# Second expert layer of a routed mixture: the last two of eight weight blocks go from float32 products to split products

## Chip, cores and metric

The kernel runs on one core of a Trainium2 chip. The metric is the device time of one execution in microseconds; a lower one is better. The kernel is one program; nothing is computed on the host but layouts.

## What is computed

The input is four images of 256 channels by 32 x 32 points, which are 4096 tokens of 256 numbers. Three layers follow each other: a convolutional self-attention per image, an eight-head attention per image, and a routed feed-forward layer. The last one, cut to what matters here:

```python
E, D, H = (8, 256, 1024)
route_prob = softmax(xt @ Wr + br)
routes = argmax(route_prob)
h = gelu(xt @ w1 + bb1)              # 256 -> 1024, by the token's own expert
y = h @ w2 + bb2                     # 1024 -> 256: the second expert layer
out = sum over experts of y * (routes == e)
x = t + out
```

The reference runs every expert on every token and masks the result; the kernel sorts the tokens by expert and runs each through its own. All of it is float32.

## The kernel before

The kernel has four phases, each of them a block in which every engine has its own stream of instructions, and which ends when all engines have come to its end.

**conv_phase** works through four images of eight blocks of 128 tokens. TensorE does the projections, the scores and the outputs, VectorE the maxima and the residuals, ScalarE the exponentials. GpSimd adds the normed rows to the residual (`a_res`, L479 and L483) once per image, and in the time left prepares the second layer's weights: `w2_load` brings a piece of 128 x 512 into one of two raw buffers (the memory of `w_qk1`, which is free once VectorE has split it; semaphore `v_wlo`), `w2_split` rounds it to `w2_hi` (type fp32r, L452), subtracts to get the low half in place (L454), and stores both halves to a scratch tensor in memory, `w2_scr`. Six of the eight 256-column blocks of each expert are prepared (`SPLIT = 6`), which is 24 pieces, six per image. `w2_hi` is one buffer: each piece waits until the one before has been stored (`w2_hi_out`). The next load waits for the low half of the other raw buffer (`w2_lo_out`).

**head_phase** works through 32 heads. At every fourth head SyncE's queue loads one expert's `w2_hi` (six blocks, from scratch) and `w2_rest` (blocks 6 and 7, from the input).

**output_phase** projects the values, adds them to the residual (`res0` to `res3`), stores the result (`t_scr`, L1458), norms it, routes it, and scatters each token's normed row to its expert's region (`rows_out`, L1400, one indirect transfer from GpSimd's queue per block of 128 tokens, 32 in all). SyncE's queue loads the low halves (`w2_lo`, L1453) and, into `res0`, the biases `b2`. Tables say which expert and which rows each tile has. Those of the first nine tiles (`READY`) are made from two images alone, so that the expert tiles can start early. At its end SyncE waits for the scatters of these two images (`ready_scattered`) and for the tables, and then issues the rows of tile 0 (`xs`, L1478), the first layer's weights of tile 0 (L1481, one transfer of 1 MB into the memory of `lnt`) and the rows of tile 1.

**expert_phase** works through 39 tiles of 128 rows. The order on TensorE is: first layer of tile i + 1 (L1984, 16 float32 matmuls that are recorded as 32), two transposes of the rows of tile i + 2 (L1973), second layer of tile i. A float32 matmul here is recorded as two. The second layer takes blocks 0 to 5 as three products of fp32r halves (high x high and high x low, L1998; low x high, L2003) and blocks 6 and 7 as float32 matmuls (L2000):

```python
for c in range(SPLIT):
    for w in (w2_hi, w2_lo):
        nc.tensor.matmul(ps_y[:, 0:C], hid_hi[k][:, c, :], of(w, c), ...)
for c in range(SPLIT, KC):
    nc.tensor.matmul(ps_y[:, 0:C], hid_t[k][:, c, :], of(w2_rest, c - SPLIT), ...)
pe.wait_ge(v_lo, i + 1)
for c in range(SPLIT):
    last = nc.tensor.matmul(ps_y[:, 0:C], hid_lo[k][:, c, :], of(w2_hi, c), ...)
```

VectorE's order per tile is: bias of the first layer's result (L1910), copy of the turned rows (`xs_c`, L1917), result `ys` of the tile before (L1928, L1935), low half of the hidden rows (`hid_lo`, L1922). Between its tiles 0 and 1 and its tiles 1 and 2 it also makes the tables of the other 30 tiles (L1333 to L1391). ScalarE does GELU (`hid`, L2035) and the high half (`hid_hi`, L2037). GpSimd gathers the residual rows and scatters the results. SyncE's queue loads rows (L1789) and 1 MB of first-layer weights per tile (L1811 for tile 1, L1795 for the others; the buffer comes free when the first layer two tiles before is done, `pe_hid`), and fills the regions' ends (L1779). All of the latter must have landed, and all scatters, before it loads tile 8.

Of the kernel before, what the change touches and what calls it, by code (L numbers as in the profile page):

```python
# [25 lines left out]
F32R = mybir.dt.float32r  # L26
# [5 lines left out]
P = 128  # L32
# [17 lines left out]
SPLIT = 6  # L50
PIECE = 2 * C
W2_PIECES = E * SPLIT * C // PIECE
# [209 lines left out]
def conv_phase(nc, io, keep, hd):  # L262
# [5 lines left out]
    with ExitStack() as ctx:  # L268
# [56 lines left out]
        w2_in, w2_lo_out = [sem(f"w2_in{k}") for k in range(2)], [sem(f"w2_lo_out{k}") for k in range(2)]  # L325
# [23 lines left out]
        with nc.Block(no_gpsimd_drain=True) as block:  # L349
# [82 lines left out]
            def _(pool):  # L432
# [8 lines left out]
                def w2_load(n):  # L441
                    e, cols = w2_piece(n)
                    pool.dma_start(w2_raw[:, n % 2, :], io["w2"][e][:, cols]).then_inc(w2_in[n % 2], 16)

                def w2_split(n):

                    k = n % 2
                    e, cols = w2_piece(n)
                    pool.wait_ge(w2_in[k], 16 * (n // 2) + 16)
                    if n:  # L450
                        pool.wait_ge(w2_hi_out, 16 * n)
                    nc.gpsimd.tensor_copy(w2_hi[:, :], w2_raw[:, k, :]).then_inc(g_whi, 1)  # L452
                    pool.wait_ge(g_whi, n + 1)
                    nc.gpsimd.tensor_tensor(w2_raw[:, k, :].bitcast(F32R), w2_raw[:, k, :], raw(w2_hi[:, :]), ALU.subtract).then_inc(g_wlo, 1)  # L454
                    pool.dma_start(io["w2_scr"][0, e][:, cols], raw(w2_hi[:, :])).then_inc(w2_hi_out, 16)
                    pool.wait_ge(g_wlo, n + 1)
                    pool.dma_start(io["w2_scr"][1, e][:, cols], w2_raw[:, k, :]).then_inc(w2_lo_out[k], 16)
# [9 lines left out]
                pool.wait_ge(v_wlo, 1)  # L467
                w2_load(0)
                w2_load(1)
                for b in range(B):  # L470
                    r = res[b % 2]
                    for n in range(b * W2_PIECES // B, (b + 1) * W2_PIECES // B):
# [18 lines left out]
                for k in range(2):  # L491
                    pool.wait_ge(w2_lo_out[k], 16 * W2_PIECES // 2)

# [488 lines left out]
def head_phase(nc, io, keep, sems, hd):  # L982


    with ExitStack() as ctx:
# [40 lines left out]
        with nc.Block(no_gpsimd_drain=True) as block:  # L1026

            @block.sync
            def _(sp):
# [3 lines left out]
                def head(t, j, first=False, left=SLOTS):  # L1033
# [3 lines left out]
                    if not first:  # L1037
# [5 lines left out]
                        if j == 2:  # L1043
                            sp.dma_start(raw(keep["w2_hi"][:, bass.ds(t, 1)]).rearrange("p o k m -> p (o k m)"),
                                         io["w2_scr"][0, bass.ds(t, 1)].rearrange("o p m -> (o p) m")).then_inc(sems["w_in"], 16)
# [357 lines left out]

def first_weights(keep):
# [4 lines left out]
def output_phase(nc, io, keep, sems):  # L1409


    with ExitStack() as ctx:
# [32 lines left out]
        with nc.Block(no_gpsimd_drain=True) as block:  # L1445

            @block.sync
            def _(sp):
                for b in range(2, B):
                    res_load(sp, io, keep, sems, b)  # L1450
                def w2_rests(experts):
                    for e in experts:
                        sp.dma_start(raw(keep["w2_lo"][:, e]).rearrange("p k m -> p (k m)"), io["w2_scr"][1, e]).then_inc(sems["lo_in"], 16)  # L1453

                w2_rests(range(6, E))
                for b in range(B):
# [6 lines left out]
                    if b == 1:  # L1463
# [5 lines left out]
                        sp.dma_start(keep["res0"][:, :, :], io["b2"].partition_broadcast(P)).then_inc(sems["bias_in"], 16)  # L1469
                table = keep["schedule"]  # L1470
# [3 lines left out]
                for k, w1 in enumerate(first_weights(keep)):  # L1474
# [242 lines left out]
def expert_phase(nc, io, keep, sems):  # L1717


    with ExitStack() as ctx:  # L1720
# [9 lines left out]
        w2_hi, w2_lo, w2_rest, prior = keep["w2_hi"], keep["w2_lo"], keep["w2_rest"], keep["prior"]  # L1730
# [7 lines left out]
        hid_hi, hid_lo = ([sb(f"hid_{x}{k}", [P, SPLIT, P], F32R) for k in range(2)] for x in ("hi", "lo"))  # L1738
# [42 lines left out]
        with nc.Block() as block:  # L1781
# [115 lines left out]
            def _(dve):  # L1897
# [21 lines left out]
                def rest(i, k):  # L1919

                    dve.wait_ge(a_hi, i + 1)
                    nc.vector.tensor_tensor(hid_lo[k][:, :, :], hid_t[k][:, 0:SPLIT, :], raw(hid_hi[k][:, :, :]), ALU.subtract).then_inc(v_lo, 1)  # L1922

# [27 lines left out]
                rest(0, 0)  # L1951
# [14 lines left out]
            def _(pe):  # L1966
# [21 lines left out]
                def second_layer(i, k, first=False):  # L1988
# [3 lines left out]
                    else:  # L1992
                        pe.wait_ge(sems["lo_in"], 16 * E)
                    of = lambda w, c: w[:, bass.ds(e, 1), c, :].rearrange("p o n -> p (o n)")
# [34 lines left out]
            def _(act):  # L2029
                def gelu(i, k, first=False):  # L2030
# [6 lines left out]
                    nc.scalar.activation(hid_hi[k][:, :, :], hid_t[k][:, 0:SPLIT, :], ACT.Copy).then_inc(a_hi, 1)  # L2037
# [12 lines left out]
def program(nc, io):  # L2050
    for n, shape in (("qk_scr", [2, 2, B * NH, D, N]),
                     ("v_scr", [P, B * NH, NB * D]), ("r_scr", [B, N, C]), ("t_scr", [B * N + P, C]), ("xs_scr", [E * REGION, C + 1]),
                     ("w2_scr", [2, E, P, SPLIT * C])):
        io[n] = nc.dram_tensor(n, shape, F32, kind="Internal").ap()
    with ExitStack() as ctx:
# [11 lines left out]
        keep["w2_hi"] = ctx.enter_context(nc.sbuf_tensor("w2_hi", [P, E, SPLIT, C], F32R))  # L2067
        keep.update(kept((("w2_rest", [P, E, KC - SPLIT, C]), ("padding", [P, C + 1]),
# [13 lines left out]
        keep["w2_lo"] = ctx.enter_context(nc.sbuf_tensor("w2_lo", [P, E, SPLIT, C], F32R))  # L2082
# [57 lines left out]
```

## Time and profile before

| | |
|---|---|
| median of 3 runs | 1191.05 us (1190.48 to 1195.1) |
| the profiled execution, its own time | 1192.07 us |
| its span, first to last instruction | 1190.2 us |
| TensorE busy | 1106.0 us, 93% |
| VectorE / GpSimd / ScalarE busy | 713.0 / 677.9 / 469.7 us |
| mean granted TensorE clock | 0.954 of 2.4 GHz |
| conv_phase | about 0 to 345 us |
| head_phase | about 345 to 832 us |
| output_phase | about 832 to 900 us |
| expert_phase | about 900 us to the end |

Times of instructions are microseconds from the start of the span. A wait is put down to what released it. Matmuls overlap in their pipeline, so the time that one takes of TensorE is the distance between the starts of two, or a group's share of the chain of work, and not the duration of one. "DMA share" is the mean busy share of the 16 DMA engines. The granted clock is told as a share of the full one.

### The profile page before, as it was taken

The numbers are of one execution on the slowest core, as the hardware profiler recorded it, in microseconds if no ns is written. First come the engines' busy times: TensorE is split into PE (matmuls) and PEld (weight loads), VectorE is DVE, ScalarE is ACT, GpSimd is POOL, SyncE is SP. The second block draws the span as 40 slices with busy tenths as digits, with TensorE's granted clock in tenths as the row PEclk, the third lists the DMA queues.
The fourth block names the chain that finished last, engine by engine and source line by source line (L and its number), as shares of the span: only waits on it lengthen the run. The fifth ranks groups of instructions, "written<-read, shape, count | busy, mean of one in ns | idle before, by whom it ended". The sixth has DMA issues, their size and how long they took to land. (4 is left out here: it accounts for less than half of the span.)

```text
span 1190.2 us, 24360 instructions
## 1 busy us (share of the span) xinstructions
PE 1106.0 (93%) x7846; PEld 817.5 (69%) x7847; DVE 713.0 (60%) x1523; ACT 469.7 (39%) x556; POOL 677.9 (57%) x686
## 2 busy tenths in 40 slices
PE   6898999899689999999999999999876999999995
PEld 3586878778455555555555555556756899999995
DVE  3265757657757777777777777760574544444442
ACT  2303232131225555555555555555551222232231
POOL 0155444263337777777777777783057455555553
PEclk8799999989779999999999999999888999999998
DMA  7335465636171323232323232314678666566561
GB/s 218 98 107 182 163 212 182 252 106 221 48 267 40 97 61 97 60 97 62 97 62 97 62 97 62 97 33 125 248 287 254 212 209 229 202 212 220 199 224 36
DMA packets 69677, 173.67 MB, mean 146 GB/s; under 512 B 12768, under 2 KB 33184, under 8 KB 68992
## 3 DMA queue, kind: packets, MB, share of 16 engines
q1 hardware_dynamic: 56336, 131.25, 34.4%
q0 software_dynamic: 13296, 41.84, 10.3%
q8 instruction: 25, 0.41, 0.1%
q14 instruction: 20, 0.16, 0.0%
HBM read 117.16 MB, written 52.45 MB: 143 GB/s over the span
## 5 line engine op out<-in xcount | busy, mean ns | idle before, releaser
L225 DVE TENSOR_REDUCE s_nmax<-ps_v 128x1 f32<-128x512 f32 x484 | 311.6, 686 | 115.9 <-PE ps_v L219 106.4
L1088 POOL TENSOR_TENSOR h_added<-h_added,h_expd 128x1024 f32<-128x1024 f32 x124 | 295.5, 2383 | 38.2 <-ACT h_expd L1111 30.4
L1111 ACT ACTIVATE h_expd<-ps_v 128x1024 f32<-128x1024 f32 x128 | 131.0, 1023 | 154.9 <-PE ps_v L1137 150.2
L1984 PE MATMUL ps_h<-xs_c,lnt 128*128 128x128 f32 x1248 | 149.4, 279 | 5.6 <-DVE xs_c L1917 3.8
L1984 PEld LDWEIGHTS ps_h<-xs_c,lnt 128*128 128x128 f32 x1248 | 146.0, 196 | 6.8 <-issue 4.1
L1151 PE MATMUL h_ps_o<-h_expd,s_vh 128*32 128x256 f32 x2048 | 137.9, 387 | 0.0
L1111 ACT ACTIVATE h_expd<-h_ps_e 128x1024 f32<-128x1024 f32 x128 | 130.4, 1018 | 0.0
L653 PE MATMUL a_ps_v<-a_val,a_expd 128*128 128x257 f32 x512 | 120.6, 389 | 5.8 <-ACT a_expd L524 4.5
L653 PEld LDWEIGHTS a_ps_v<-a_val,a_expd 128*128 128x128 f32 x512 | 98.5, 194 | 24.3 <-ACT a_expd L524 6.5
L2035 ACT ACTIVATE hid<-ps_h 128x1024 f32<-128x1024 f32 x39 | 39.9, 1024 | 188.4 <-DVE ps_h L1910 188.4
L1838 POOL TENSOR_TENSOR pause<-pause 128x1 f32<-128x1 f32 x156 | 53.2, 341 | 103.6 <-DVE ys L1935 92.6
L1088 POOL TENSOR_TENSOR h_added<-h_expd 128x1024 f32<-128x1024 f32 x31 | 73.8, 2380 | 56.4 <-ACT h_expd L1111 56.4
L1910 DVE TENSOR_TENSOR ps_h<-ps_h,b_t 128x1024 f32<-128x1024 f32 x39 | 48.1, 1233 | 87.0 <-PE ps_h L1984 85.6
L1151 PEld LDWEIGHTS h_ps_o<-h_expd,s_vh 128*32 128x32 f32 x2048 | 53.7, 109 | 51.9 <-issue 22.5
L802 DVE TENSOR_REDUCE a_nmax<-a_ps_m 128x1 f32<-128x512 f32 x64 | 41.2, 685 | 63.4 <-PE a_ps_m L613 63.4
L452 POOL CAST a_w_hi<-a_w_qk 128x512 fp32r<-128x512 f32 x24 | 14.7, 614 | 94.7 <-DMA a_w_qk<-in_w 89.9
L1998 PE MATMUL ps_y<-w_hi,hid_hi 128*128 x234 | 60.6, 296 | 0.6 <-DVE ys L1935 0.6
L1400 POOL DMA_INDIRECT xs_scr<-lnt,pos x32 | 31.2, 975 | 46.3 <-DVE pos L1687 37.5
L1998 PE MATMUL ps_y<-w_lo,hid_hi 128*128 x234 | 57.4, 282 | 0.0
L219 PE MATMUL ps_v<-s_stk2m,s_stk2n 96*128 96x512 f32 x128 | 52.3, 457 | 2.3 <-issue 2.3
L219 PE MATMUL ps_v<-s_stk3m,s_stk3n 96*128 96x512 f32 x128 | 51.6, 447 | 0.0
L1935 DVE TENSOR_TENSOR ys<-ps_y,t_rows 128x256 f32<-128x256 f32 x39 | 16.6, 425 | 51.9 <-PE ps_y L2003 50.2
(258 smaller groups left out, 2018.1 us busy)
## 6 DMA issues: line engine op xcount, KB each, us to landing
lnt<-in_w SPq DMA_DIRECT2D x39, 1024.0 KB, 4.9
qk_scr<-a_head_hi SPq DMA_DIRECT2D x14, 512.0 KB, 4.0
qk_scr<-a_head_lo SPq DMA_DIRECT2D x14, 512.0 KB, 5.5
a_w_qk<-in_w POOLq DMA_DIRECT2D x24, 256.0 KB, 4.0
w_scr<-a_w_hi POOLq DMA_DIRECT2D x24, 256.0 KB, 2.5
w_scr<-a_w_qk POOLq DMA_DIRECT2D x24, 256.0 KB, 3.1
w_hi<-w_scr SPq DMA_DIRECT2D x8, 768.0 KB, 4.4
w_lo<-w_scr SPq DMA_DIRECT2D x8, 768.0 KB, 9.9
```

What stands on the lines that cost most here:

```text
L219: self.nc.tensor.matmul(ps_m[:, half, :], n_st[0:STACK, nb * P:(nb + 1) * P], m_st[0:STACK, half * HALF:(half + 1) * HALF], start=True, st ...
L225: self.nc.vector.tensor_reduce(self.nmax[k][:, nb, half:half + 1], ps_m[:, half, :], AX.X, ALU.max, negate=True).then_inc(self.v_max, 1)
L653: last = nc.tensor.matmul(ps_v[:, j % 2, 0:C + 1], expd[:, m, j * P:(j + 1) * P], val[b % 2][:, m, :], start=(m == 0), stop=(m == NB - 1))
L802: nc.vector.tensor_reduce(nmax[b % 2][:, nb, half:half + 1], ps_m[:, half, :], AX.X, ALU.max, negate=True).then_inc(v_max, 1)
L1088: nc.gpsimd.tensor_tensor(total[:, :], (expd[:, 0, :] if m == 1 else total[:, :]), expd[:, m, :], ALU.add).then_inc(g_add, 1)
L1111: nc.scalar.activation(expd[:, m, :], flat(ps_e[m % 2]), ACT.Exp, scale=SCALE).then_inc(a_exp, 1)
L1151: mm = nc.tensor.matmul(ps_o[j % 2][q * D:(q + 1) * D, 0:QUARTER], vh[j % SLOTS][:, m, :], expd[:, m, q * QUARTER:(q + 1) * QUARTER], star ...
L1838: nc.gpsimd.tensor_tensor(pause[:, n:n + 1], pause[:, 0:1], pause[:, 0:1], ALU.add)
L1910: nc.vector.tensor_tensor(blocks, blocks, b1_t[:, bass.ds(e, 1), :].rearrange("p o (k n) -> p (o k) n", n=1).to_broadcast([P, KC, P]), ALU ...
L1984: last = nc.tensor.matmul(ps_h[k][:, c // 4, c % 4 * P:(c % 4 + 1) * P], w1_now[k][:, t, c * P:(c + 1) * P], xs_c[:, t, :], start=(t == 0) ...
L1998: nc.tensor.matmul(ps_y[:, 0:C], hid_hi[k][:, c, :], of(w, c), start=(c == 0 and w is w2_hi), stop=False)
L2035: nc.scalar.activation(hid_t[k].rearrange("p k n -> p (k n)"), flat(ps_h[k]), ACT.Gelu).then_inc(a_gelu, 1)
```

## The change

All eight blocks of the second layer become split products: the float32 matmuls on `w2_rest` are gone, and blocks 6 and 7 take part in the two loops of fp32r products. For that

- GpSimd prepares 32 pieces instead of 24, nine for each of the first two images, then eight and six. It has a third raw buffer (the memory of `w_v1`), starts with three loads when VectorE has split both weights, and loads two pieces ahead.
- In head_phase the transfer of `w2_rest` becomes one of `w2_hi_rest`, of the same size, from scratch.
- The low halves of blocks 6 and 7 are two more transfers of 1 MB on SyncE's queue in output_phase. One goes into `res1`, behind the store of image 2, once image 1 has been normed. The other goes into `vals_c`, behind the rows of tile 1 and ahead of the first-layer weights of tile 1. Both are made of runs of 1 KB.
- `hid_hi` and `hid_lo` have eight blocks; `hid_lo` has one buffer, and VectorE waits for the second layer before (`pe_ys`) ahead of writing it.

```diff
-SPLIT = 6
+LO_KEPT = 6
-W2_PIECES = E * SPLIT * C // PIECE
+W2_PIECES = E * KC * C // PIECE
+W2_OF_IMAGE = (9, 9, 8, 6)
...
+        w2_raws = [w2_raw[:, 0, :], w2_raw[:, 1, :], w_v1[:, :, :].rearrange("p t m -> p (t m)")]
...
-                    if n and n + 1 < W2_PIECES:
-
-                        pool.wait_ge(w2_lo_out[1 - k], 16 * ((n + 1) // 2))
-                        w2_load(n + 1)
+                    if n and n + 2 < W2_PIECES:
+
+                        pool.wait_ge(w2_lo_out[(n - 1) % 3], 16 * ((n - 1) // 3 + 1))
+                        w2_load(n + 2)
...
-                pool.wait_ge(v_wlo, 1)
-                w2_load(0)
-                w2_load(1)
+                pool.wait_ge(v_wlo, 2)
+                for n in range(3):
+                    w2_load(n)
...
-                            sp.dma_start(keep["w2_rest"][:, bass.ds(t, 1)].rearrange("p o k m -> p (o k m)"),
-                                         io["w2"][bass.ds(t, 1)][:, :, SPLIT * C:KC * C].rearrange("o p m -> (o p) m")).then_inc(sems["w_in"], 16)
+                            sp.dma_start(raw(keep["w2_hi_rest"][:, bass.ds(t, 1)]).rearrange("p o k m -> p (o k m)"),
+                                         io["w2_scr"][0, bass.ds(t, 1)][:, :, LO_KEPT * C:KC * C].rearrange("o p m -> (o p) m")).then_inc(sems["w_in"], 16)
...
+                def w2_block(dst, c):
+
+                    sp.dma_start(dst, io["w2_scr"][1][:, :, c * C:(c + 1) * C].rearrange("e p m -> p e m")).then_inc(sems["lo_in"], 16)
...
+                    if b == 2:
+
+                        sp.wait_ge(a_ln, 4)
+                        w2_block(keep["res1"][:, :, :], LO_KEPT)
...
+                sp.wait_ge(pe_pr, 2 * B)
+                w2_block(by_block(vals_c), LO_KEPT + 1)
                 sp.wait_ge(t_stored, 16 * B)
...
-        hid_hi, hid_lo = ([sb(f"hid_{x}{k}", [P, SPLIT, P], F32R) for k in range(2)] for x in ("hi", "lo"))
+        hid_hi = [sb(f"hid_hi{k}", [P, KC, P], F32R) for k in range(2)]
+        hid_lo = sb("hid_lo", [P, KC, P], F32R)
...
-                    for c in range(SPLIT):
-                        for w in (w2_hi, w2_lo):
-                            nc.tensor.matmul(ps_y[:, 0:C], hid_hi[k][:, c, :], of(w, c), start=(c == 0 and w is w2_hi), stop=False)
-                    for c in range(SPLIT, KC):
-                        nc.tensor.matmul(ps_y[:, 0:C], hid_t[k][:, c, :], of(w2_rest, c - SPLIT), start=False, stop=False)
+                    for c in range(KC):
+                        nc.tensor.matmul(ps_y[:, 0:C], hid_hi[k][:, c, :], hi(c), start=(c == 0), stop=False)
+                        nc.tensor.matmul(ps_y[:, 0:C], hid_hi[k][:, c, :], lo(c), start=False, stop=False)
                     pe.wait_ge(v_lo, i + 1)
-                    for c in range(SPLIT):
-                        last = nc.tensor.matmul(ps_y[:, 0:C], hid_lo[k][:, c, :], of(w2_hi, c), start=False, stop=(c == SPLIT - 1))
+                    for c in range(KC):
+                        last = nc.tensor.matmul(ps_y[:, 0:C], hid_lo[:, c, :], hi(c), start=False, stop=(c == KC - 1))
```

## Rows read from the trace of the kernel before

**Rows 1.** The page: busy time of each engine, share of the span, instructions.

```profile
PE 1106.0 (93%) x7846; PEld 817.5 (69%) x7847; DVE 713.0 (60%) x1523; ACT 469.7 (39%) x556; POOL 677.9 (57%) x686
```

**Rows 2.** The chain that ended last, one later tile: start, us, what.

```profile
1041.07 1.43 PE ps_y L1998 x12
1042.50 0.86 PE ps_y L2000 x4
1043.36 0.71 PE ps_y L2003 x6
1044.08 3.57 PE ps_h L1984 x32
```

**Rows 3.** Groups of instructions, 900 to 1190 us: busy us, mean ns, idle before.

```profile
L2035 ACT ACTIVATE hid<-ps_h 128x1024 f32<-128x1024 f32 x39 | 39.9, 1024 | 188.4 <-DVE ps_h L1910 188.4
...
L1922 DVE TENSOR_TENSOR hid_lo<-hid,hid_hi 128x768 fp32r<-128x768 f32 x39 | 37.0, 950 | 4.7 <-ACT hid_hi L2037 4.7
...
L2037 ACT ACTIVATE hid_hi<-hid 128x768 fp32r<-128x768 f32 x39 | 33.0, 845 | 1.2
```

**Rows 4.** The same chain, asked for 896 to 966 us.

```profile
896.14 6.16 DMA lnt<-in_w
...
902.39 5.55 PE ps_h L1984 x32
...
917.26 0.86 DVE hid_lo L1922
...
924.27 0.85 ACT hid_hi L2037
...
925.15 0.96 DVE hid_lo L1922
...
932.90 5.47 PE ps_h L1984 x32
...
948.70 5.83 DMA xs_scr<-padding
...
956.85 5.22 DMA lnt<-in_w
```

**Rows 5.** Timeline of TensorE, two first layers: start, us, idle before and releaser.

```profile
909.77 3.81 PE L1984 MATMUL ps_h<-xs_c,lnt 128*128 128x128 f32 x32 [1.63 <-DVE xs_c L1917]
...
932.90 1.31 PE L1984 MATMUL ps_h<-xs_c,lnt 128*128 128x128 f32 x6 [2.22 <-DVE xs_c L1917]
```

**Rows 6.** Stretches: length, busy time by engine, granted clock, DMA share, GB/s.

```profile
888.00:890.00 2.00, 1.87 (x11) 1.17 (x9) 1.59 (x11) 1.59 (x4) 1.70 (x2) 0.77 1.07 392
...
902.00:907.00 5.00, 4.61 (x26) 4.64 (x27) 0.00 (x0) 0.00 (x0) 3.06 (x6) 0.60 0.91 285
...
932.00:938.00 6.00, 5.10 (x31) 5.10 (x32) 2.56 (x5) 1.86 (x2) 3.45 (x8) 0.72 0.31 115
```

**Rows 7.** Waits of SyncE's queue: waiting line, releaser, total us, times, longest.

```profile
SPq L1473 <- DVE tab_start_i L1370: 13.2, 1, 13.2
```

**Rows 8.** L1400 (scatters), those that started between 882 and 885 us.

```profile
DMA to landing us min/median/max: 6.2/6.5/6.5
```

**Rows 9.** L1400, the two at 887.86 and 889.13 us, last of image 1.

```profile
DMA to landing us min/median/max: 4.2/4.4/4.6
```

**Rows 10.** Timeline and transfers of SyncE's queue: first-layer weights of tile 1.

```profile
900.79 0.38 SPq L1811 DMA_DIRECT2D lnt<-in_w  x1
...
lnt<-in_w SPq DMA_DIRECT2D x1, 1024.0 KB, 7.9
```

**Rows 11.** Timeline of conv_phase, around the first image's end: GpSimd, TensorE, ScalarE.

```profile
87.15 0.61 POOL L452 CAST a_w_hi<-a_w_qk 128x512 fp32r<-128x512 f32 x1 [3.35 <-DMA a_w_qk<-in_w]
...
95.20 0.76 PEld L638 LDWEIGHTS a_ps_e<-a_stk1n,a_stk1m 98*128 98x128 f32 x4 [0.81 <-DMA a_stk1n<-a_mrow]
...
98.52 4.54 POOL L479 TENSOR_TENSOR a_res<-a_res,a_lnt 128x2048 f32<-128x2048 f32 x1 [7.84 <-DVE a_lnt L127]
...
126.30 1.20 ACT L540 ACTIVATE a_h_hi<-a_ps_e,a_gab 128x1024 fp32r<-128x1024 f32 x1 [18.16 <-DVE a_gab L888]
```

More of the change, by code:

```diff
@@ L324, in conv_phase @@
         w2_hi = sb("w2_hi", [P, PIECE], F32R)
-        w2_in, w2_lo_out = [sem(f"w2_in{k}") for k in range(2)], [sem(f"w2_lo_out{k}") for k in range(2)]
+        w2_raws = [w2_raw[:, 0, :], w2_raw[:, 1, :], w_v1[:, :, :].rearrange("p t m -> p (t m)")]
+        w2_in, w2_lo_out = [sem(f"w2_in{k}") for k in range(3)], [sem(f"w2_lo_out{k}") for k in range(3)]
         w2_hi_out, g_whi, g_wlo = sem("w2_hi_out", "g_whi", "g_wlo")
@@ L466, in _ @@
                 pool.wait_ge(consts_in, all_consts)
-                pool.wait_ge(v_wlo, 1)
-                w2_load(0)
-                w2_load(1)
+                pool.wait_ge(v_wlo, 2)
+                for n in range(3):
+                    w2_load(n)
                 for b in range(B):
                     r = res[b % 2]
-                    for n in range(b * W2_PIECES // B, (b + 1) * W2_PIECES // B):
+                    for n in range(sum(W2_OF_IMAGE[:b]), sum(W2_OF_IMAGE[:b + 1])):
                         w2_split(n)
@@ L490, in _ @@
                 pool.wait_ge(w2_hi_out, 16 * W2_PIECES)
-                for k in range(2):
-                    pool.wait_ge(w2_lo_out[k], 16 * W2_PIECES // 2)
+                for k in range(3):
+                    pool.wait_ge(w2_lo_out[k], 16 * len(range(k, W2_PIECES, 3)))
             @block.scalar
@@ L1401, in rows_out, with by_block @@
                                 keep["lnt"][:, i, :], None).then_inc(done, 16)
+def by_block(t):
+    return t[:, :, :].rearrange("p t n -> p (t n)").rearrange("p (e m) -> p e m", m=C)
 def first_weights(keep):
@@ L1728, in sem @@
             return ctx.enter_context(nc.semaphore(name))
-        w2_hi, w2_lo, w2_rest, prior = keep["w2_hi"], keep["w2_lo"], keep["w2_rest"], keep["prior"]
+        w2_hi, w2_lo, w2_hi_rest, prior = keep["w2_hi"], keep["w2_lo"], keep["w2_hi_rest"], keep["prior"]
+        w2_lo_rest = [t.bitcast(F32R) for t in (keep["res1"][:, :, :], by_block(keep["vals_c"]))]
         ident = keep["ident"]
@@ L1917, in tokens, with rest @@
                     nc.vector.tensor_copy(xs_c[:, :, :], ps_x[:, 0:C].rearrange("p (t n) -> p t n", t=CT)).then_inc(v_xs, 1)
-                def rest(i, k):
+                def rest(i, k, first=False):
                     dve.wait_ge(a_hi, i + 1)
-                    nc.vector.tensor_tensor(hid_lo[k][:, :, :], hid_t[k][:, 0:SPLIT, :], raw(hid_hi[k][:, :, :]), ALU.subtract).then_inc(v_lo, 1)
+                    if not first:
+                        dve.wait_ge(pe_ys, i)
+                    nc.vector.tensor_tensor(hid_lo[:, :, :], hid_t[k][:, :, :], raw(hid_hi[k][:, :, :]), ALU.subtract).then_inc(v_lo, 1)
                 def result(i, k, nth, first):
@@ L1950, in _ @@
                 tokens(1)
-                rest(0, 0)
+                rest(0, 0, first=True)
                 tile(0, first=True)
@@ L1992, in second_layer @@
                     else:
-                        pe.wait_ge(sems["lo_in"], 16 * E)
-                    of = lambda w, c: w[:, bass.ds(e, 1), c, :].rearrange("p o n -> p (o n)")
+                        pe.wait_ge(sems["lo_in"], 16 * (E + 2))
+                    row = lambda w: w[:, bass.ds(e, 1)].rearrange("p o n -> p (o n)")
+                    hi = lambda c: row(w2_hi[:, :, c, :] if c < LO_KEPT else w2_hi_rest[:, :, c - LO_KEPT, :])
+                    lo = lambda c: row(w2_lo[:, :, c, :] if c < LO_KEPT else w2_lo_rest[c - LO_KEPT])
                     pe.wait_ge(a_hi, i + 1)
-                    for c in range(SPLIT):
-                        for w in (w2_hi, w2_lo):
-                            nc.tensor.matmul(ps_y[:, 0:C], hid_hi[k][:, c, :], of(w, c), start=(c == 0 and w is w2_hi), stop=False)
-                    for c in range(SPLIT, KC):
-                        nc.tensor.matmul(ps_y[:, 0:C], hid_t[k][:, c, :], of(w2_rest, c - SPLIT), start=False, stop=False)
+                    for c in range(KC):
+                        nc.tensor.matmul(ps_y[:, 0:C], hid_hi[k][:, c, :], hi(c), start=(c == 0), stop=False)
+                        nc.tensor.matmul(ps_y[:, 0:C], hid_hi[k][:, c, :], lo(c), start=False, stop=False)
                     pe.wait_ge(v_lo, i + 1)
-                    for c in range(SPLIT):
-                        last = nc.tensor.matmul(ps_y[:, 0:C], hid_lo[k][:, c, :], of(w2_hi, c), start=False, stop=(c == SPLIT - 1))
+                    for c in range(KC):
+                        last = nc.tensor.matmul(ps_y[:, 0:C], hid_lo[:, c, :], hi(c), start=False, stop=(c == KC - 1))
                     last.then_inc(pe_ys, 1)
@@ L2036, in gelu @@
                     act.wait_ge(a_gelu, i + 1)
-                    nc.scalar.activation(hid_hi[k][:, :, :], hid_t[k][:, 0:SPLIT, :], ACT.Copy).then_inc(a_hi, 1)
+                    nc.scalar.activation(hid_hi[k][:, :, :], hid_t[k][:, :, :], ACT.Copy).then_inc(a_hi, 1)
                 def tile(i, parity=0, first=False, next_tile=True, ahead=True):
@@ L2066, in program @@
             "ready_scattered", "xs_in", "w1_in0", "w1_in1", "pe_vt", "pe_pr", "a_vt", "res_in0", "res_in1", "res_in2", "res_in3", "table_in", "bias_in")}
-        keep["w2_hi"] = ctx.enter_context(nc.sbuf_tensor("w2_hi", [P, E, SPLIT, C], F32R))
-        keep.update(kept((("w2_rest", [P, E, KC - SPLIT, C]), ("padding", [P, C + 1]),
+        keep["w2_hi"] = ctx.enter_context(nc.sbuf_tensor("w2_hi", [P, E, LO_KEPT, C], F32R))
+        keep["w2_hi_rest"] = ctx.enter_context(nc.sbuf_tensor("w2_hi_rest", [P, E, KC - LO_KEPT, C], F32R))
+        keep.update(kept((("padding", [P, C + 1]),
                           ("res1", [P, NB, C]), ("w_pr", [P, CT, C]), ("w_rt", [P, CT, D]), ("b_rt", [P, E]),
```

20 lines of the change are left out of this document (10 added, 10 removed).

## The prediction

> **What bounds the kernel now.** I read the page first: TensorE is busy 93% of the span [rows 1], so the question for any edit is where TensorE waits, and for whom. Then the chain of work that ended last. From about 962 us to the end it is TensorE alone: per tile 12 products of halves, 4 records of float32, 6 more products of halves, then the next tile's first layer [rows 2]. From one first layer to the next it is 6.79 us, the four rows and 0.22 us of transposes; nothing else is on it, and ScalarE stands idle 4.9 us per tile (188.4 us over 39) [rows 3]. Before 962 us the chain changes hands [rows 4]: the transfer of the first weights (896.14, 6.16 us), TensorE, VectorE with its tables from 916.8 to 932.4 us, TensorE, then SyncE's padding (5.83 us) and the weights behind it (5.22 us). So the first nine tiles have other limits than the last thirty, and each term must be read in its own place. In conv_phase GpSimd, which gets more work, waits in every piece and before each `a_res` [rows 11].
>
> **The second layer's own time.** A product of halves takes 1.43 / 12 = 0.119 us; the 6 low products take 0.71, the same. The two float32 blocks take 0.86 us [rows 2]. Removed: 0.86. Added: 6 products, 6 x 0.119 = 0.715. The gain is 0.145 us per tile. It counts where TensorE is on the chain: second layers 7 to 38 (32 of them), and those of tiles 0 and 3, which lead to VectorE's tables and to SyncE's padding. Those of tiles 1 and 2 lie under the tables, and those of 4, 5 and 6 beside SyncE's padding and the load behind it, whose length TensorE doesn't set [rows 4]. 34 x 0.145 = 4.9 us gained. Bounds: 3.4 us if a product with its new addresses takes 0.127, 5.7 us if all 39 count.
>
> Here a page and the rows differ. The rows price a float32 block at 0.43 us, that is 3.6 products of halves [rows 2]. The Trainium skill ("FP8 and Floating Point Precision", section "TensorE Precision Notes") says that true float32 goes through the array in four passes; three products of one pass would then save a quarter of 0.43, which is 0.215 us per tile and 7.3 us over 34. The rows don't show that: a product costs 0.119 us and not a quarter of 0.43, 0.107.
>
> **Eight blocks on ScalarE and VectorE.** `hid_lo` has 768 elements in 950 ns and gets 1024: 0.95 x 4/3 is 1.27, so +0.3 at most. `hid_hi` has 845 ns; GELU over 1024 takes 1024 ns, so +0.2 [rows 3]. In the later tiles both are hidden: ScalarE has 4.9 us of idle time per tile to take 0.2 from, and `hid_lo` is asked for only after 16 products (1.9 us) of the second layer. The new wait for `pe_ys` comes behind `result`, which waits for the same event already; nothing new queues behind it. Between 916 and 932 us they are on the chain: `hid_lo` twice, `hid_hi` once [rows 4], so 2 x 0.3 + 0.2 = 0.8 us lost (0.6 to 0.8).
>
> **The 1 MB into `res1`.** VectorE and ScalarE don't need it, but it lengthens the queue. The DMA engines are full until about 890 us (392 GB/s) [rows 6], with low halves, biases and two stores in SyncE's queue. 1 MB at that rate is 2.7 us more of it. Who is late: scatters take 6.2 to 6.5 us to land while the queue is full [rows 8]. The last one that tile 0 waits for (889.13 us) landed in 4.6, as the queue ran dry [rows 9], at 893.7; SyncE went on at 893.9, when the tables came [rows 7]. With a full queue it lands at 895.5, and everything behind is 1.6 us later. I take 1.5 (0 if the store of image 3 finishes as before, 1.9 at most).
>
> **The 1 MB into `vals_c`.** It is issued after the rows of tile 1 (897.4 us before) and ahead of the weights of tile 1, issued at 900.79, which took 7.9 us [rows 10] and landed at 908.7. The first layer of tile 1 began at 909.77, on VectorE's copy [rows 5], so there are 1.1 us to spare. The queue moved 285 GB/s then with a share of 0.91 [rows 6]: 1 MB ahead is 3.7 us at that rate, 2.7 at 392. I take 3.3, as part of the scatters will be done, less 1.1: 2.2 us of a new wait of TensorE (1.6 to 2.6, and 0.5 if the traffic has thinned). It isn't needed itself before the second layer of tile 0, over 10 us later. The weights of tiles 2 and 3 follow behind it in the same queue, but the tables have the chain there, with about 4 us over.
>
> **The clock behind that wait.** The first layer of tile 0 took 5.55 us and that of tile 4 5.47 us, against 3.57 later [rows 2, 4]. Their stretches have a granted clock of 0.60 and 0.72 [rows 6], a mean of the half level (1.2 GHz) and the full one. Tile 4 came after 2.22 us of idle TensorE; tile 1 came after 1.63 us and took 3.81 [rows 5]. With a wait of 2.2 us on top the idle time before tile 1 is 3.8 us, nearer to tile 4's. I count 5.5 - 3.8 = 1.7 us (0 to 1.7).
>
> **GpSimd in conv_phase.** Eight pieces more. A piece had 3.35 us of idle waiting for its load [rows 11]; with two loads ahead that goes, and what remains is some 3.6 us of work and issuing or the store of `w2_hi`, so I estimate 4.5 to 5 us a piece for 6.9. Nine pieces then take about what six took. If none of it came true, nine at 6.9 would end 3 x 6.9 = 21 us later, less the 7.8 us that `a_res` waited: 13 us late, and ScalarE asks for it 23 us after its end (103.1 to 126.3) [rows 11]. What can leak through is traffic: the two small rows that TensorE waits for at 95.20 us had no pieces beside them and now may. I take 0.5 us over the four images (-0.5 to 3). head_phase moves the same bytes by the same number of issues: 0.
>
> **The sum.** -4.9 + 0.8 + 1.5 + 2.2 + 1.7 + 0.5 = +1.8 us. Against the profiled execution (1192.07, of which 1.9 lie around the span of 1190.2) this is 1193.9; the median is 1.0 lower than that execution, so 1192.9. With every term at its low end: -5.7 + 0.6 + 0 + 0.5 + 0 - 0.5 = -5.1, 1186.0. At its high end: -3.4 + 0.8 + 1.9 + 2.6 + 1.7 + 3 = +6.6, 1197.7.
>
> **Rivals.**
> A. The start costs nothing. The scatter lands in time, tile 1's weights find a thinner queue, no wait and no clock loss. For it: only 1.1 us of the block's time has to be absorbed, and the barrier at 900 us, not the queue, sets the issue of tile 1's weights. Against it: shares of 0.9 and 1.07 [rows 6]. Then -4.9 + 0.8 + 0.5 = -3.6: 1187.5.
> B. A product of halves costs a quarter of the float32 block's 0.43 us [rows 2] in the two new blocks, so 3 save 0.107 each block and 0.215 per tile, and the start is cheap: -7.3 + 0.8 + 0 to 0.5 = -6.3: 1184.8, beyond 0.5%. Against it stands the row of 0.119 us.
> C. GpSimd's eight further pieces slow VectorE in conv_phase. Each has about 1.9 us of GpSimd reading the same memory; if every subtraction (1.3 us) held up a VectorE instruction on TensorE's path, that is 10 us, so 1201 with the rest. It decides from about five of the eight on (+6 us in all). Against: the maxima, VectorE's largest group there, read the other memory, and the 24 pieces of before leave no wait with GpSimd's name before TensorE.
> D. The start is worse: w1 transfers stay one block late until tile 4, the tables are overtaken, and the clock falls twice (+1.7 again, +2): +5.5 in all, 1196.6.
>
> **Chances.** Forecast 0.43, A 0.27, B 0.06, C 0.09, D 0.15. 0.5% is 6 us and is about what a measurement of this kernel can tell from no change. Faster by more: B and a tail of A, 0.09. Slower by more: C, a part of D, 0.17. Within: 0.74. The forecast's own range is 1189 to 1196; to hold 8 in 10 it must reach A and D: 1186 to 1198.5.
>
> **What would show it.** In the steady tiles 24 products at 0.119 us and a tile of 6.64 us instead of 6.79; `hid_lo` near 1.25 us. SyncE's line before tile 0's rows released by a scatter and no more by the tables. The first layer of tile 1 released by its weights, more than 2.5 us idle before it, and 5 us or more long. Tile 4's first layer some 6 us later against tile 0's issue point. `a_res` of the first image still waiting for VectorE. Wrong if tile 1 starts without a wait, if the product's time changes, or if conv_phase ends more than 3 us later.

## The result and the profile after

The changed kernel takes 1195.77 us (median of 20 runs, 1191.21 to 1201.81) beside 1191.05 us for the kernel before (20 runs, 1186.25 to 1196.44). The ratio is 1.0039, 95% interval [1.0025, 1.0053]: about 4.6 us slower. The interval excludes 1, so the kernel is slower clear of noise, though by less than the 0.5% that I had called no change; the interval's upper end is just above that. The profiled execution took 1193.73 us, its span 1191.9.

The page's row of busy time after the change:

```profile
PE 1096.2 (92%) x7924; PEld 812.3 (68%) x7925; DVE 728.5 (61%) x1523; ACT 478.5 (40%) x556; POOL 726.7 (61%) x726
```

TensorE is busy 9.8 us less than in [rows 1] and the span is still 1.7 us longer, so it waits 11.5 us more. The chain in one later tile of the changed kernel (start, us, what):

```profile
1021.84 3.57 PE ps_h L2004 x32
1025.41 0.22 PE ps_x L1993 x2
1025.62 0.12 PE ps_y L2019
1025.74 0.12 PE ps_y L2020
...
1027.51 0.95 PE ps_y L2023 x8
1028.47 0.56 PE ps_h L2004 x5
```

From one first layer to the next it is 6.63 us (1028.47 - 1021.84) instead of 6.79 [rows 2]. The groups of the later tiles, 970 to 1185 us:

```profile
L1942 DVE TENSOR_TENSOR hid_lo<-hid,hid_hi 128x1024 fp32r<-128x1024 f32 x31 | 38.0, 1226 | 0.2 <-ACT hid_hi L2057 0.2
L2057 ACT ACTIVATE hid_hi<-hid 128x1024 fp32r<-128x1024 f32 x31 | 32.8, 1058 | 1.0
L2055 ACT ACTIVATE hid<-ps_h 128x1024 f32<-128x1024 f32 x31 | 31.8, 1026 | 141.4 <-DVE ps_h L1928 141.4
```

`hid_lo` and `hid_hi` grew by 0.28 and 0.21 us against [rows 3], and ScalarE still waits 4.6 us per tile. The start of the expert stage, the same chain:

```profile
891.45 5.79 DMA xs_scr<-lnt,pos
...
897.26 0.49 SPq L1489
...
898.25 0.35 SPq L1492
...
899.39 8.45 DMA lnt<-in_w
...
907.93 5.47 PE ps_h L2004 x32
```

SyncE is now released by the last scatter (L1489 waits for `xs_scr`), where the tables released it before [rows 7]. Then the first weights, which landed in 6.16 us before [rows 4], take 8.45. TensorE's timeline, the first layers of tiles 0, 1 and 4 (idle before them and releaser in brackets):

```profile
907.93 5.46 PE L2004 MATMUL ps_h<-xs_c,lnt 128*128 128x128 f32 x32 [4.05 <-DMA lnt<-in_w]
915.24 3.81 PE L2004 MATMUL ps_h<-xs_c,lnt 128*128 128x128 f32 x32 [1.63 <-DVE xs_c L1935]
...
939.06 5.28 PE L2004 MATMUL ps_h<-xs_c,lnt 128*128 128x128 f32 x32 [2.76 <-DVE xs_c L1935]
```

The row of tile 1 is that of [rows 5] to the hundredth: the wait that I forecast there isn't there. SyncE's queue around the two new transfers (L1463):

```profile
873.07 10.83 SPq L1463 DMA_DIRECT2D res<-w_scr  x1
883.94 4.05 SPq L1468 DMA_DIRECT2D t_scr<-c_res  x1
...
901.53 0.34 SPq L1492 DMA_DIRECT2D xs<-xs_scr  x1
901.92 0.56 SPq L1463 DMA_DIRECT2D vals_c<-w_scr  x1
903.75 0.38 SPq L1829 DMA_DIRECT2D lnt<-in_w  x1
```

The two DMA rows of `res1` and of image 3's store took 10.83 and 4.05 us to issue, at a DMA share of 1.02 from 873 to 884 us; I read that as a full queue, which no run isolates. In the kernel before, image 3's store was issued in 2.06 us (878.62), 3.3 us behind VectorE's last residual; here that issue ends 8.6 us behind it. In conv_phase, GpSimd's timeline shows pieces 4.8 us apart (87.69 to 92.50) instead of 6.9 [rows 11], and the residual of the first image still waits for VectorE:

```profile
87.69 0.61 POOL L454 CAST a_w_hi<-a_w_qk 128x512 fp32r<-128x512 f32 x1 [0.84 <-DMA w_scr<-a_w_hi]
...
92.50 0.61 POOL L454 CAST a_w_hi<-a_w_v 128x512 fp32r<-128x512 f32 x1 [1.29 <-DMA w_scr<-a_w_hi]
...
98.50 4.55 POOL L481 TENSOR_TENSOR a_res<-a_res,a_lnt 128x2048 f32<-128x2048 f32 x1 [2.46 <-DVE a_lnt L128]
```

### The profile page after: what moved, and what is told of

The parts are those of the page before. It is cut to its first block and busy times, and to the rows that moved or that the text cites. A ratio compares the mean times of both kernels' runs of the same rounds, so it can differ in the third digit from the quotient of the medians.

```text
span 1191.9 us, 24683 instructions
## 1 busy us (share of the span) xinstructions
PE 1096.2 (92%) x7924; PEld 812.3 (68%) x7925; DVE 728.5 (61%) x1523; ACT 478.5 (40%) x556; POOL 726.7 (61%) x726
## 5 line engine op out<-in xcount | busy, mean ns | idle before, releaser
L1856 POOL TENSOR_TENSOR pause<-pause 128x1 f32<-128x1 f32 x156 | 68.3, 438 | 85.0 <-DVE ys L1955 73.1
L1942 DVE TENSOR_TENSOR hid_lo<-hid,hid_hi 128x1024 fp32r<-128x1024 f32 x39 | 47.8, 1227 | 5.8 <-ACT hid_hi L2057 5.8
```

Source lines behind the costliest of these rows:

```text
L1856: nc.gpsimd.tensor_tensor(pause[:, n:n + 1], pause[:, 0:1], pause[:, 0:1], ALU.add)
L1942: nc.vector.tensor_tensor(hid_lo[:, :, :], hid_t[k][:, :, :], raw(hid_hi[k][:, :, :]), ALU.subtract).then_inc(v_lo, 1)
```

## The experiments

Three stretches, in us, by which single profiles can be compared; each number is from one profile, and only the kernel before has two. "Conv" is from the first product behind the first image's small row of maxima to the start of the fourth image's last part, less the time that the granted clock took away in it (the sum over slices of 1 us of one less the granted clock). "Start" is from VectorE's last residual of output_phase to tile 0's first layer. "Steady" is from the first layer of tile 8 to the end.

| kernel | conv | start | steady |
|---|---|---|---|
| before; a second profile of it (f3) | 251.0; 250.5 | 25.0; 25.1 | 227.9; 228.0 |
| changed | 255.0 | 28.5 | 223.4 |
| e1, e2, e3, e4 | 255.5, 254.5, 252.5, 254.3 | 28.3, 28.5, 28.0, 28.4 | 223.4, 223.2, 223.4, 228.3 |
| f1, f2 | 253.5, 250.9 | 24.6, 28.2 | 227.7, 227.6 |
| f4 | 259.8 | 28.1 | 227.9 |
| g1, g2, g3, g4 | 250.4, 250.9, 253.7, 253.8 | 26.2, 24.7, 28.9, 24.9 | 227.6, 227.7, 223.5, 223.4 |

**e1: the transfer into `vals_c` behind tile 1's weights.**

```diff
-                sp.wait_ge(pe_pr, 2 * B)
-                w2_block(by_block(vals_c), LO_KEPT + 1)
...
                 sp.dma_start(w1_now[1], ...).then_inc(w1_in[1], 16)
+                sp.dma_start(by_block(keep["vals_c"]), ...block 7...).then_inc(sems["lo_in"], 16)
```

> The changed kernel, but the 1 MB into vals_c is issued behind the first-layer weights of tile 1 and not ahead of them. Theory (the block's bytes are moved between those of tile 0's weights and slow them): those weights land 6.2 us after issue again and not 8.45, tile 0's first layer starts 2.3 us earlier against the marker of conv_phase's end; the bytes come back behind tile 1 at most in part, since VectorE's tables have the chain there. Net -1 to -2.3 us against the changed kernel. Rival (tile 0's weights are late for another reason, such as the scatters, which now run at the same time as them): they still take 8 us or more, and nothing is gained.

Measured: 1195.22 us, ratio 1.0036 [1.0017, 1.0055]. The chain:

```profile
887.33 5.76 DMA xs_scr<-lnt,pos
...
895.25 8.33 DMA lnt<-in_w
903.67 5.29 PE ps_h L2003 x32
```

With nothing of mine in the queue behind it, the first transfer of weights takes 8.33 us all the same. The block in front of tile 1's weights was not what made it late. This profile is of the fastest of e1's twelve runs. That this profile's whole output stage is 3 us shorter comes earlier, from a stretch of low clock that this execution doesn't have (from the first residual to the last 41.3 us instead of 44.0, and 41.3 in f2, which lacks it too), and not from the edit.

**e2: neither transfer.**

```diff
-                        w2_block(keep["res1"][:, :, :], LO_KEPT)
-                w2_block(by_block(vals_c), LO_KEPT + 1)
+                    lo = lambda c: row(w2_lo[:, :, c if c < LO_KEPT else c - LO_KEPT, :])
```

> The changed kernel without either 1 MB transfer; blocks 0 and 1 of the low halves stand in for 6 and 7, so the low halves of two blocks are wrong. Everything else stays. Theory (the two transfers cost all of the delay between output_phase and tile 0's first layer, 0.85 us by the scatter that lands late and 2.3 us by the weights): from the first residual of output_phase to tile 0's first layer it is 69.5 us as before the change and not 72.5, so -3 us against the changed kernel, and SyncE is released by the tables again. Rival (part of it comes from elsewhere): more than 70.5 us remain.

Measured: 1194.79 us, 1.0027 [1.0006, 1.0048]. The last scatter lands 0.7 us sooner than in the changed kernel, but the weights take longer still:

```profile
891.97 5.06 DMA xs_scr<-lnt,pos
...
899.46 8.92 DMA lnt<-in_w
```

So the late start outlives both transfers that I had blamed for it.

**e3: 24 pieces on the three buffers.**

```diff
-W2_PIECES = E * KC * C // PIECE
+W2_PIECES = E * LO_KEPT * C // PIECE
-W2_OF_IMAGE = (9, 9, 8, 6)
+W2_OF_IMAGE = (6, 6, 6, 6)
```

> The changed kernel with 24 pieces, six per image, on the three raw buffers; the halves of blocks 6 and 7 are taken from blocks 0 and 1, by transfers of the same size, so the second layer is wrong in two blocks. Theory (GpSimd's eight further pieces cost conv_phase 2.4 us, by VectorE's short instructions that are held up by GpSimd's and by the small rows of maxima that land behind pieces): the mark at the end of conv_phase, GpSimd's first memset of head_phase, is back at 342 us from 344.6, and the short VectorE instructions of the norms at 161 ns from some 360. Rival (the third buffer and the tighter pace do it, not the number): 344 us or more remain.

Measured: 1196.14 us, 1.0042 [1.0026, 1.0058]. The small rows of maxima come as before (3.8 us from the product that turns them to the first score product, 4.7 and 4.5 in the changed kernel), and conv is 2.5 us shorter at full clock; the median shows none of it.

**e4: the changed kernel with float32 matmuls for blocks 6 and 7 on TensorE, on the high halves alone; all else kept.**

```diff
-                    for c in range(KC):
+                    for c in range(LO_KEPT):
...
+                    for c in range(LO_KEPT, KC):
+                        nc.tensor.matmul(ps_y[:, 0:C], hid_t[k][:, c, :], raw(hi(c)), ...)
```

> The changed kernel in all its preparation, transfers, ScalarE and VectorE work, but TensorE takes blocks 6 and 7 as float32 matmuls again, on the high halves of the weights alone, so their low halves are left out. Theory (the gain is TensorE's 0.145 to 0.16 us per tile and nothing else in the steady tiles changed): the tile takes 6.79 us again, from tile 8's first layer to the end it is 227.9 us instead of 223.4, and the whole is 4.5 to 5 us slower than the changed kernel. Rival (the tiles would have become slower or faster by the rest, such as the wider hid_lo and hid_hi): a tile differs from 6.79 us.

Measured: 1201.0 us, 1.0076 [1.0051, 1.0101], 5.2 us above the changed kernel by the medians and 4.4 by the ratios. Its chain has the old rows back, 0.86 for the two blocks and 0.72 for six low products:

```profile
1042.13 0.86 PE ps_y L2022 x4
1042.99 0.72 PE ps_y L2025 x6
1043.70 3.57 PE ps_h L2004 x32
```

From tile 8 to the end it is 228.3 us instead of 223.4. The gain of the steady tiles is TensorE's alone.

**f1: the kernel before with the third raw buffer and loads two ahead, still 24 pieces.** Its diff is that of `w2_raws`, `w2_load` and `w2_split` in the change.

> The kernel before, with the third raw buffer and loads two pieces ahead, still 24 pieces; nothing else of the change. In the changed kernel and three variants of it the part that is not steady tiles is 8 to 9 us dearer by the medians than before, whether or not the eight further pieces or the two 1 MB transfers are in. Theory P (the tighter pace of GpSimd's pieces holds up VectorE and shortens nothing): slower than before by 2 to 4 us, in conv_phase. Theory N (conv_phase differs from execution to execution by stretches of low clock, and the pace costs nothing): within 1 us of before.

Measured: 1194.74 us, 1.0029 [1.0014, 1.0044], so +3.4 us, for an edit that makes GpSimd's pieces shorter and touches nothing behind 345 us. One of VectorE's groups of short norm instructions in conv_phase (45 to 300 us; times, busy us, mean ns), first the kernel before:

```profile
L92 DVE SCALAR_TENSOR_TENSOR a_rstd<-a_tmp,a_rstd 128x2 f32<-128x2 f32 x9 | 1.4, 161 | 0.3
```

then the kernel with the third buffer:

```profile
L92 DVE SCALAR_TENSOR_TENSOR a_rstd<-a_tmp,a_rstd 128x2 f32<-128x2 f32 x9 | 2.4, 267 | 0.3
```

and the changed kernel:

```profile
L93 DVE SCALAR_TENSOR_TENSOR a_rstd<-a_tmp,a_rstd 128x2 f32<-128x2 f32 x9 | 3.4, 374 | 0.3
```

Same tile, same work, and the mean doubles. Over all instructions of this helper in the stretch (63, in f1 58) the mean is 164 ns in each of the five profiles with 24 pieces on two buffers, 203 in f1 and 242 in the changed kernel (+4.9 us in all). The timeline of f1 from 125 us on shows what holds them up, and who waits behind:

```profile
125.68 1.26 POOL L455 TENSOR_TENSOR a_w_v<-a_w_v,a_w_hi 128x512 fp32r<-128x512 f32 x1
125.84 1.12 DVE L92 SCALAR_TENSOR_TENSOR a_rstd<-a_tmp,a_rstd 128x2 f32<-128x2 f32 x1
...
128.79 1.10 PE L614 MATMUL a_ps_m<-a_stk0m,a_stk0n 96*128 96x512 f32 x2 [0.48 <-DVE a_nmax L803]
```

A VectorE instruction that takes 0.16 us elsewhere takes 1.12 and ends with GpSimd's subtraction (126.96 and 126.94). The maxima behind it (`a_nmax`) come late, and TensorE's second pair of products for them waits for VectorE, which it doesn't in the kernel before. This norm stands at three places of the conv stretch. There the second pair comes 4.69, 4.68 and 4.59 us behind the first, instead of 4.07, 3.87 and 3.87: 2.2 of the 2.5 us by which conv grew.

**f2: the kernel before with the two 1 MB transfers, nothing using them.** The diff is that of `w2_block` and its two calls.

> The kernel before, with two transfers of 1 MB at the two places where the changed kernel has them, into res1 and vals_c (blocks 0 and 1 of the low halves, not used). Theory B (these two cost the start of expert_phase 3 to 4 us): slower by 3 to 4 us, with 72 to 72.5 us from the first residual of output_phase to tile 0's first layer against 69.5. Rival (the variant of the changed kernel without them took as long, so they cost about 1 us): within 1.5 us of before.

Measured: 1194.79 us, 1.0032 [1.0019, 1.0045], so +3.8 us. The start is 3.1 us longer: the last scatter lands in 6.81 us and the weights in 7.36.

**f3: the kernel before once more, for a second profile.**

> The kernel before once more, for a second profile of it. If the stages differ by themselves, conv_phase ends anywhere from 341 to 345 us and the first layer of tile 0 comes 69.5 to 72.5 us after the first residual of output_phase; if the first profile is typical, both lie within 0.5 us of 342.2 and 69.5.

Measured: 1189.19 us. Its span is 2.9 us shorter than that of the first profile, 2.2 of it in the stretch from 43 to 303 us, mostly clock; start and steady tiles agree to 0.1 us. One profile against one can't show 2 us in conv_phase unless the clock is taken out first.

**f4: the kernel before with 32 pieces, eight for each image, still on two buffers.**

> The kernel before, with 32 pieces on its two raw buffers, eight per image, rows of the scratch tensor eight blocks long; the halves of blocks 6 and 7 are made and not used. Theory W (the further pieces themselves cost, by traffic and by VectorE held up): slower by 2 to 3 us, in conv_phase. Theory N: within 1 us of before.

Measured: 1217.43 us, 1.0222 [1.0197, 1.0246], so +26 us. GpSimd's timeline:

```profile
89.62 0.61 POOL L452 CAST a_w_hi<-a_w_qk 128x512 fp32r<-128x512 f32 x1 [4.42 <-DMA a_w_qk<-in_w]
...
96.23 0.61 POOL L452 CAST a_w_hi<-a_w_qk 128x512 fp32r<-128x512 f32 x1 [3.09 <-DMA a_w_qk<-in_w]
...
108.43 4.51 POOL L479 TENSOR_TENSOR a_res<-a_res,a_lnt 128x2048 f32<-128x2048 f32 x1
```

The pieces wait for their loads, and `a_res` comes 10 us later and with no wait in front: GpSimd has become the bound. In the profile the conv stretch is 18.6 us longer, 8.8 of them at full clock; the clock took away 18.4 us in it, for 8.5 in the kernel before. Another 3.0 are the start. So what takes out the low clock takes out a part of the price as well where TensorE waits this much, and the third buffer's +3.4 us buys off some 19. This profile is also the first sign of what e2 left open: its second layer is the old one and it has neither transfer, yet its start is 28.1 us. What it shares with e1 to e4 is a scratch with rows of eight blocks, of which six are read.

**g1: the kernel before, rows of eight blocks in the scratch, six of them used.**

```diff
-                     ("w2_scr", [2, E, P, SPLIT * C])):
+                     ("w2_scr", [2, E, P, KC * C])):
-                        sp.dma_start(raw(keep["w2_lo"][:, e])..., io["w2_scr"][1, e])
+                        sp.dma_start(raw(keep["w2_lo"][:, e])..., io["w2_scr"][1, e][:, 0:SPLIT * C])
```

> The kernel before with one edit: a row of the scratch for the halves has eight blocks (8 KB) of which six are written and read, so the transfers of low and high halves read 6 KB out of every 8 KB. The first weights of the expert stage took 5.8 to 6.3 us to land in the three profiles whose scratch has rows of six blocks and no transfer beside them, and 8.2 to 8.9 us in the five whose scratch has rows of eight, with or without the two 1 MB transfers. Theory that the scratch alone does it (its rows or its place in memory): landing of 8.3 us or more, the first layer of tile 0 about 28.3 us behind VectorE's last residual of image 3 instead of 25.0, and a ratio of 1.001 to 1.003. Rival, that it is the wider second layer or the number of pieces: 6.2 us, 25.0 us, a ratio of 1.

Measured: 1192.13 us, 1.0004 [0.9987, 1.0022].

```profile
890.91 5.43 DMA xs_scr<-lnt,pos
...
898.50 6.78 DMA lnt<-in_w
```

The tables no longer release SyncE, a scatter does, and the start is 1.2 us longer, not 3.3: the sign of the theory, a third of its size, and too little for the ratio to tell from nothing.

**g2: the kernel before, scratch larger by an unused third part (`[3, E, P, SPLIT * C]`).**

> The kernel before with one edit: the scratch is 50% larger, by a third part that nothing uses; rows of six blocks as before. If the 6 KB out of 8 KB are what delays the first weights, these land after 6.2 us here and the time is that of before (ratio within 0.1% of 1). If it is where the scratch and what lies behind it stand in memory, they take 8.3 us here too, and the first layer of tile 0 is 3 us later.

Measured: 1191.4 us, 0.9994 [0.9978, 1.0011]; weights in 5.84 us, start 24.7. A larger scratch, with what it moves behind it, doesn't matter.

**g3: the changed kernel, blocks 6 and 7 in a scratch of their own.**

```diff
-                     ("w2_scr", [2, E, P, KC * C])):
+                     ("w2_scr", [2, E, P, LO_KEPT * C]), ("w2_end", [2, E, P, (KC - LO_KEPT) * C])):
```

> The changed kernel with its scratch in two: rows of six blocks as in the kernel before, and a second scratch for blocks 6 and 7 of both halves (2 KB rows). The two 1 MB transfers stay in their places. Theory of the rows: the first weights land in about 7.4 us (as with the two transfers alone added to the kernel before) instead of 8.45, and the profiled span is 1 to 2 us shorter: a ratio of 1.002 to 1.003 to the kernel before. Rival, place or size: 8.4 us, and a ratio of 1.004 as the changed kernel has.

Measured: 1194.45 us, 1.0033 [1.0016, 1.0049]; weights in 7.83 us where I expected about 7.4, but SyncE got past the scatters 1 us later than in the changed kernel, and the start is no shorter (28.9). Its conv is 253.7 us with the helper's norm instructions at 164 ns; the same hold-up stands a few instructions further on, ending with GpSimd's at 126.58 and 126.57:

```profile
125.31 1.26 POOL L463 TENSOR_TENSOR a_w_v<-a_w_v,a_w_hi 128x512 fp32r<-128x512 f32 x1
125.46 1.12 DVE L897 TENSOR_TENSOR a_gab<-a_gnw,a_tmp 128x2 f32<-128x2 f32 x1
...
127.24 1.10 PE L622 MATMUL a_ps_m<-a_stk0m,a_stk0n 96*128 96x512 f32 x2 [0.50 <-DVE a_nmax L811]
```

**g4: g3 with both transfers behind tile 1's weights and eight pieces for each image.**

> The changed kernel with the scratch in two, both 1 MB transfers behind the first-layer weights of tile 1, and eight pieces for each image instead of 9, 9, 8, 6. By the theories of the scratch's rows, of the transfers and of the small rows of maxima, this takes 2.8 us off the time to tile 0 and 1 to 1.5 us off the convolutional stage; left against the kernel before are the third buffer's +3.4 and the tables' +0.7 against -4.5 in the steady tiles: about -0.4 us, a ratio of 0.9985 to 1.001, and the first version that isn't slower than before. If the start is set by something else it stays at 1.003.

Measured: 1199.56 us, 1.0061 [1.0038, 1.0084], the worst of the versions with the new second layer on TensorE, where I expected the best. TensorE's timeline:

```profile
911.12 5.55 PE L2003 MATMUL ps_h<-xs_c,lnt 128*128 128x128 f32 x32 [1.35 <-DMA lnt<-in_w]
...
918.52 3.81 PE L2003 MATMUL ps_h<-xs_c,lnt 128*128 128x128 f32 x32 [1.63 <-DVE xs_c L1934]
925.54 0.69 PE L1992 MATMUL ps_x<-ident,xs 128*128 128x128 f32 x2 [3.21 <-DMA xs<-xs_scr]
```

and its chain:

```profile
906.18 7.30 DMA xs<-xs_scr
...
914.28 11.22 DMA xs<-xs_scr
```

The start is whole again (24.9 us, the wait for the weights 1.35). But the 128 rows of tile 2 stand behind 2 MB in SyncE's queue, take 11.22 us to land, and TensorE waits for them; the second layer behind that wait runs at half the pace (0.21 us a product). From tile 1 to tile 4 it is 30.1 us instead of 23.8. Less 3.6 us at the start and more 6.3 here is 2.7 us of the 3.8 by which it is slower than the changed kernel. The rest isn't shown: this profile is of the slowest of g4's six runs, and the clock took 11.9 us of its conv stretch, where it took 6.8 of the changed kernel's.

## Why the prediction was right

The total was 2.9 us low and inside the range, with two of its terms wrong in opposite directions: that the total came out is in part luck. One of my own signs of being wrong came true, as tile 1 started without the new wait. Another sign failed too: tile 4's first layer came 2.9 us later against the issue of tile 0's rows (40.8 for 37.9), not 6. The conv stretch is 2.3 us longer as the profiles stand and 4.1 with the clock taken out. By the prediction's own steps:

- **The second layer's own time, -4.9 us: right.** The tile takes 6.63 us for the 6.64 forecast, a product 0.118 us (1.89 / 16). From tile 8 to the end the kernels with float32 blocks take 227.6 to 228.3 us and the others 223.2 to 223.4, so 4.5 us for the 4.6 that belong to that stretch (32 second layers). Rival B, and with it the reading of the Trainium skill ("FP8 and Floating Point Precision", section "TensorE Precision Notes") as four times the price of one pass, is out: the trace prices a float32 block at 3.6 products, and nothing near 7.3 us was gained.
- **Eight blocks on ScalarE and VectorE, +0.8: right.** 1.23 and 1.06 us; from tile 1 to tile 4 it is 23.8 us instead of 23.1.
- **The 1 MB into `res1`, +1.5: right.** SyncE issued tile 0's rows 1.2 us later behind VectorE's last residual in the changed kernel and in e1, which has only this transfer there, and 1.9 and 2.2 in f2 and g3. The size isn't this transfer's alone, as e2 without it is still 0.6 us late.
- **The 1 MB into `vals_c`, +2.2, and the clock behind it, +1.7: wrong in its place and too large.** This step failed. Tile 1 had 1.63 us of idle time and took 3.81, as before. I had taken 1.1 us of spare time before tile 1 as fixed, but it isn't: when tile 0 is late, so is all that tile 1 needs from the other engines. Its weights, 10.0 us on the way, landed 1.5 us before it began. What was late was the first transfer of weights, +2.3 us, ahead of the block, and e1 shows that it is late without the block. Nor was there a clock to lose where the wait came: tile 0's first layer took 5.55 us before and 5.47 after, at a granted clock of 0.67 and 0.68, and tile 1's had the full one in both.
- **What lengthens the start is shown only in part.** It is 24.6 to 25.1 us in the five profiles with neither a 1 MB transfer in output_phase nor a scratch read six blocks out of eight; 26.2 to 28.5 with such a scratch alone (g1, f4, e2); 28.2 and 28.9 with the transfers alone (f2, g3); 28.0 to 28.5 with both. In the changed kernel undoing one gains nothing (e2, g3) and undoing both gains all of it (g4): there either will do it, and they don't add. In the kernel before, the scratch alone costs 1.2 us (g1); what makes it 3.0 in f4, which has 32 pieces besides, isn't shown. Both hold up the last scatter: tile 0's rows are issued 0.6 to 0.7 us late with the scratch alone, 1.9 and 2.2 with the transfers alone. Why the weights then take 0.6 to 2.8 us more stays open. It isn't traffic just ahead of them: over the 5 us before their issue the DMA share is 0.93 in the changed kernel, but 0.36 in e2 as it is 0.35 in the kernel before. Nor is it, in most, a want of DMA engines: from 1 to 3 us behind their issue the share is 0.59 in the changed kernel and 0.53 to 0.60 in g1, g3, f4 and e2 (0.77 in f2, 0.94 in e1), and 0.97 in the kernel before, which is the faster one. First the kernel before, then the changed one (length, busy by engine, granted clock, DMA share, GB/s):

```profile
897.14:899.14 2.00, 0.46 (x3) 0.27 (x2) 0.98 (x4) 0.00 (x0) 1.58 (x2) 0.50 0.97 254
```

```profile
900.39:902.39 2.00, 0.00 (x0) 0.00 (x0) 1.23 (x6) 0.00 (x0) 1.70 (x2) 0.50 0.59 122
```

- **GpSimd in conv_phase, +0.5 (-0.5 to 3): wrong, mis-sized and past its bound.** With the clock taken out, conv is 250.4 to 251.0 us for the five profiles with 24 pieces on two buffers, 252.5 and 253.5 for the two with 24 on three, 253.7 to 255.5 for the six with 32 on three: +2.2 us for the pace and 1.5 more for the pieces. f1 has +3.4 us for the pace alone by its median. I had the pace right (4.8 us) and `a_res` too, and looked only at what a late GpSimd could delay, not at what a quicker one does to its neighbours. That was rival C, which I gave 10 us and 0.09: its mechanism is there, at a third of the size. I had argued against it that no wait before TensorE bore GpSimd's name. None does now: a held-up VectorE instruction shows as a longer one, and TensorE's wait bears VectorE's name. The Trainium skill ("SBUF — State Buffer", section "SBUF: two separate sides") says that a VectorE instruction with two inputs in this memory and a GpSimd instruction that reads it hold the shared ports by turns, each for its whole length. The rows of f1 and g3 agree: 1.12 us instead of 0.16, ending with GpSimd's subtraction. The small rows of maxima are another 0.7 to 0.9 us each where nine pieces reach the image's end.
- **Slips in the working.** Rival C's 1201 leaves out the other terms of the forecast, with which it is 1202.4. ScalarE's 188.4 us over 39 tiles are 4.8, not 4.9. Neither changes the forecast.

Summed from the profiles: -4.5 + 0.7 + 3.5 (start) + 3.7 (conv, six profiles against five) = +3.4 us, the lower part of the measured interval of 3.0 to 6.3. The forecast had -4.9 + 0.8 + 5.4 + 0.5: the start 1.9 too high, conv 3.2 too low. What was right is the sum, the steady tiles, the tables and that the scatters come late; how the first weights and GpSimd behaved was not.

Not tried: one transfer behind tile 1's weights and the other behind tile 2's rows, which g4 suggests. Even that would keep conv_phase's 3.7 us against 4.5 gained, so I don't claim a version faster than the kernel before.

## What to carry to other kernels

A slower helper that stays off the path can be cheaper than a quick one: before taking its waits away, list the short instructions of the other engines that work on the same memory beside it, look at their durations and not only at the waits, and price the pace and not only the end. A transfer "moved to where there is room" delays whatever stands behind it in its queue, and the smallest transfer there (here 128 rows) may be the first one missed. When two causes each suffice for a delay, undoing one shows nothing; undo both before calling either innocent.

## What the runs showed that I had not expected

- The granted clock falls in stretches of about 3.5 us at the half level, which cost 1.7 us each, after a TensorE wait of only 1.1 us, and the same program has them in some profiles and not in others. In f1, slices of 1 us (length, busy by engine, granted clock, DMA share, GB/s):

```profile
180.00:181.00 1.00, 1.00 (x3) 0.88 (x4) 0.00 (x0) 0.00 (x0) 0.86 (x1) 0.67 1.04 252
181.00:182.00 1.00, 1.00 (x3) 0.73 (x3) 0.00 (x0) 0.00 (x0) 1.00 (x3) 0.50 1.09 254
182.00:183.00 1.00, 1.00 (x4) 0.81 (x3) 0.00 (x0) 0.00 (x0) 0.92 (x2) 0.50 0.91 242
183.00:184.00 1.00, 1.00 (x5) 0.78 (x4) 0.00 (x0) 0.00 (x0) 1.00 (x2) 0.63 1.04 414
```

  In the conv stretch the five profiles with 24 pieces on two buffers lost 6.8 to 10.2 us to low clock, the eight with three buffers 6.8 to 11.9, and f4 18.4.
- One DMA issue on SyncE took 10.8 us, and 10.3 to 11.9 in the five other profiles with a transfer in that place, at a DMA share of 1.02 in the changed kernel. The next issue stands behind it on the engine.
- 128 rows of 1 KB took 2.2 us to land from an empty queue and 11.2 us behind 2 MB in the same one (g4).
